# The start of a two-layer kernel on one core: first chunks in halves, products of zeros in TensorE's first waits, and adapter A turned later

## The reference

```
W_b = W0^T + coeff_b * (2 * mask_b - 1)            mask_b: 1024 x 1024 of 0 and 1
y   = x + x W_b + b0
out = y + y W1^T + b1 + (y A_b^T) B_b^T            A_b: 16 x 1024, B_b: 1024 x 16, chosen by ids[b]
```

## Time and profile before

| | us |
|---|---|
| median of 3 runs | 411.49 (410.44 to 413.1) |
| the profiled execution | 411.09 |
| its span, first to last instruction | 409.3 |
| TensorE busy | 396.6 |
| VectorE busy | 283.1 |
| ScalarE busy | 183.8 |

### The profile page before, as it was taken

How to read it: one execution, slowest core, us unless ns; L and a number is a source line. 1 busy time by engine, 2 the same in 40 slices (tenths; PEclk the granted TensorE clock), 3 DMA queues, 4 the chain that set the end, 5 groups by cost and what they waited for, 6 DMA issues and landing times.

```text
span 409.3 us, 6109 instructions
## 1 busy us (share of the span) xinstructions
PE 396.6 (97%) x2358; PEld 364.1 (89%) x2358; DVE 283.1 (69%) x343; ACT 183.8 (45%) x294; POOL 27.4 (7%) x42
## 2 busy tenths in 40 slices
PE   4899999999999999999999999999999999999995
PEld 3787788899999999999999999999999999999994
DVE  1667978867876688577886679575986679575622
ACT  3565675543444344344444345353444334353322
POOL 2224121000001000010001000010001000000000
PEclk9999999999999999999999999999999999999999
DMA  8999986259531893159531893249731793246002
GB/s 282 267 284 270 272 220 172 73 151 254 150 102 57 200 246 98 58 141 246 166 103 56 200 217 110 75 129 216 200 98 49 197 232 107 88 130 168 0 2 103
DMA packets 93633, 63.33 MB, mean 155 GB/s; under 512 B 3612, under 2 KB 90916, under 8 KB 93605
## 3 DMA queue, kind: packets, MB, share of 16 engines
q1 hardware_dynamic: 93586, 62.95, 58.3%
q10 hardware_dynamic: 18, 0.00, 0.0%
HBM read 51.39 MB, written 8.39 MB: 146 GB/s over the span
## 4 chain that ended last, share of the span: by engine, by line
PE 95%; DMA 2%; SPq 1%; DVE 1%; issue 0%; POOL 0%; ACT 0%; DVEq 0%
PE ps L756 29%; PE ps L758 15%; PE ps L802 13%; PE ps L801 13%; PE ps L800 13%; PE ps L734 4%; DMA w0raw<-in_L_cond_W_dram 2%; PE ps L780 2%; PE ps L778 2%; PE ps L779 2%; PE ps L829 2%; PE ps L766 1%; PE ps L811 0%; DVE wm L589 0%; POOL w0raw L341 0%
## 5 line engine op out<-in xcount | busy, mean ns | idle before, releaser
L756 PE MATMUL ps<-xhl,whi 128*128 128x512 f32 x512 | 184.8, 399 | 0.0
L758 PE MATMUL ps<-xhl,wlo 128*128 128x256 f32 x512 | 143.4, 280 | 0.0
L756 PEld LDWEIGHTS ps<-xhl,whi 128*128 128x128 f32 x512 | 96.5, 188 | 20.0 <-DVE xhl L579 0.4
L800 PE MATMUL ps<-w1hi,yhl 128*128 128x344 f32 (+1 forms) x336 | 108.1, 322 | 0.0
L802 PE MATMUL ps<-w1hi,yhl 128*128 128x344 f32 (+1 forms) x336 | 107.7, 321 | 0.0
L801 PE MATMUL ps<-w1lo,yhl 128*128 128x344 f32 (+1 forms) x336 | 107.6, 320 | 0.0
L596 DVE SCALAR_TENSOR_TENSOR wlo<-wm,cs_minus,whi 128x1024 fp32r<-128x1024 f32 x64 | 81.6, 1274 | 25.3 <-ACT whi L421 25.2
L758 PEld LDWEIGHTS ps<-xhl,wlo 128*128 128x128 f32 x512 | 97.0, 189 | 0.3
L421 ACT ACTIVATE whi<-wm,cs_minus 128x1024 fp32r<-128x1024 f32 x64 | 73.7, 1152 | 43.0 <-DVE wm L589 42.9
L589 DVE SCALAR_TENSOR_TENSOR wm<-wm,cs_twice,w0t 128x1024 f32<-128x1024 int32 x64 | 83.8, 1310 | 10.3 <-ACT w0t L402 8.4
L447 ACT ACTIVATE ysum<-ps,b0col 128x256 f32<-128x256 f32 x64 | 30.3, 474 | 85.5 <-PE ps L758 85.3
(11 more groups left out here) (68 smaller groups left out, 217.3 us busy)
## 6 DMA issues: line engine op xcount, KB each, us to landing
wm<-in_mask_Bx4096x_ik_dram SPq DMA_DIRECT2D x64, 512.0 KB, 4.4
xraw<-in_x_dram SPq DMA_DIRECT2D x28, 256.0 KB, 5.8
w0raw<-in_L_cond_W_dram SPq DMA_DIRECT2D x8, 512.0 KB, 7.2
w1raw<-_L_cond_base_weight_dram SPq DMA_DIRECT2D x8, 512.0 KB, 7.4
out_dram<-zst SPq DMA_DIRECT2D x20, 172.0 KB, 2.1
bt<-bhl SPq DMA_DIRECT2D x48, 64.0 KB, 2.3
out_dram<-zst SPq DMA_DIRECT2D x8, 176.0 KB, 2.2
out_dram<-zst SPq DMA_DIRECT2D x8, 164.0 KB, 2.2
```

The source lines that it names most:

```text
L756: nc.tensor.matmul(ps[:, bank, :], whi[:, s, k, :], xhl[:, b % 2, k, :], start=(k == 0), stop=False, skip_group_check=True)
L758: op = nc.tensor.matmul(ps[:, bank, 0:S], wlo[:, s, k, :], xhl[:, b % 2, k, 0:S], start=False, stop=(k == KT - 1), skip_group_check=True)
L800: nc.tensor.matmul(dst, hi, w1hi[:, c, cols], start=(c == 0), stop=False, skip_group_check=True)
```

## The change

- Chunks 0 and 1 are made, rounded and their remainder taken in two halves of 512 columns each (half_make_w, half_chunk_hi, half_chunk_lo), and layer1(0) and (1) wait for each half by itself.
- Twelve products of zeros, 128x128 by 128x512, are issued on TensorE: 5 first, then 2, 2 and 3 between the transposes of the start. Nobody reads them.
- The mask of chunk 0 is loaded ahead of both row blocks of x. The slab W1(0) is turned within chunk 1 of layer 1 and no longer ahead of it, and the order of W1, A, B, the masks, x of batch 1 and the bias on SP's queue changes.
- A is turned at the end of step 2, and adapter_h(0) and (1) run in the middle of layer1(3). B is turned in steps 4 and 5, in place of 3 and 4. A's rows lie in the memory of bt (araw), which GpSimd clears after A has been turned, and the bias is moved after that; B has a tensor of its own (braw).
- y_parts of chunk 2 comes in step 3. The second half of the rows of batch 1 is turned at the end of step 6 and its lo part taken in step 7, ahead of make_y(7).

The diff, cut to its changed lines:

```diff
-         ("w0", 1, 0, 0), ("w0", 1, 1, 1), ("w1", 0, 0, 2), ("w1", 0, 1, 3)]
+         ("w0", 1, 0, 0), ("w0", 1, 1, 1), ("w1", 0, 0, 2), ("w1", 0, 1, 3), ("w0", 2, 0, TB[0]), ("w0", 2, 1, TB[1])]
 for n in range(1, KT):
-    if n + 1 < KT:
+    if 1 < n < KT - 1:
...
+    if n in (4, 5):
+        units.append(("b", 0, n - 4, TB[1]))
+    units += [("w1", n, h, TB[h]) for h in range(2)]
     if n == 2:
-        units += [("a", 0, 0, TB[1]), ("a", 0, 1, HB)]
-    if n in (3, 4):
-        units.append(("b", 0, n - 3, TB[1]))
-    units += [("w1", n, h, TB[h]) for h in range(2)]
+        units += [("a", 0, 0, HB), ("a", 0, 1, TB[0])]
...
 def first_split(st, g):
...
+def first_lo_split(st, g):
+    return 2 * g + st + 1
...
 def l1_bank(n):
...
+    xt_at = nc.sbuf_base
...
+    zeros = nc.alloc_sbuf_tensor_at("zeros", [P, HALF], F32R, offset=xt_at)
...
-    abraw = sb("abraw", [P, D])
+    braw = sb("braw", [P, D])
+    bt_at = nc.sbuf_base
...
+    araw = nc.alloc_sbuf_tensor_at("araw", [P, D], F32, offset=bt_at)
...
         def load_a(adapters):
...
-                sp.dma_start(abraw[e * R:(e + 1) * R, :], src).then_inc(a_in, 16)
+                sp.dma_start(araw[e * R:(e + 1) * R, :], src).then_inc(a_in, 16)
...
         def load_b(adapters):
-            sp.wait_ge(unit_turned, number["a", 0, 1] + 1)
...
-                sp.dma_start(abraw[:, e * P:(e + 1) * P], src).then_inc(b_in, 16)
+                sp.dma_start(braw[:, e * P:(e + 1) * P], src).then_inc(b_in, 16)
...
         def move_bias():
-            sp.wait_ge(consts_set, 1)
+            sp.wait_ge(consts_set, 3)
...
-        sp.dma_start(xrows[:, 0, :], x[0, 0:P, :]).then_inc(rows_in[0], 16)
...
-        sp.dma_start(xrows[:, 1, :], x[0, P:2 * P, :]).then_inc(rows_in[1], 16)
+        for st in range(ST):
+            sp.dma_start(xrows[:, st, :], x[0, st * P:(st + 1) * P, :]).then_inc(rows_in[st], 16)
...
+        load_w1(1)
...
-        load_w1(1)
-        load_a(range(0, 2))
...
+        load_w1(2)
+        load_a(range(0, 4))
...
-        load_a(range(2, 5))
-        load_w1(2)
-        load_a(range(5, NB))
+        load_a(range(4, NB))
...
+            if n == 0:
+                load_b(range(NB))
             if n == 1:
+                load_x(1)
...
-                load_b(range(NB))
-                load_x(1)
...
+        nc.gpsimd.memset(zeros[:, :].bitcast(F32), 0.0).then_inc(consts_set, 1)
+        nc.gpsimd.memset(ht[:, :].bitcast(F32), 1.0).then_inc(consts_set, 1)
...
-        nc.gpsimd.memset(bt[:, :].bitcast(F32), 0.0).then_inc(consts_set, 1)
-        nc.gpsimd.memset(ht[:, :].bitcast(F32), 1.0).then_inc(consts_set, 1)
...
+        eye_w0(4)
...
-        eye_w0(4)
+        pool.wait_ge(unit_turned, number["a", 0, 1] + 1)
+        nc.gpsimd.memset(bt[:, :].bitcast(F32), 0.0).then_inc(consts_set, 1)
...
-                              abraw[:, :].rearrange("p (b o r) -> p o b r", b=NB, o=KT)).then_inc(b_sorted, 1)
+                              braw[:, :].rearrange("p (b o r) -> p o b r", b=NB, o=KT)).then_inc(b_sorted, 1)
...
         def chunk_hi(n):
...
-            if n == 0:
-                act.wait_ge(coeff_made, 2)
...
+        def half_chunk_hi(n, g):
+            if g == 0:
+                act.wait_ge(first_made, n + 1)
+            else:
+                act.wait_ge(w_made, n + 1)
+            k = slice(g * TG, (g + 1) * TG)
+            op = nc.scalar.activation(whi[:, n, k, :], wm[:, n, g * HALF:(g + 1) * HALF].rearrange("p (k o) -> p k o", k=TG),
+                                      ACT.Identity, bias=cs_minus[:, 0:1])
+            if g == 0:
+                op.then_inc(first_hi, 1)
+            else:
+                op.then_inc(w_hi, 1)
...
         def rows_hi(b, g):
...
+        act.wait_ge(coeff_made, 2)
+        half_chunk_hi(0, 0)
...
+        half_chunk_hi(0, 1)
...
-        chunk_hi(0)
...
-        chunk_hi(1)
+        half_chunk_hi(1, 0)
+        half_chunk_hi(1, 1)
...
+            if n == 3:
+                y_parts_hi(2)
...
-            if n == 2:
-                split_hi("a", 0, 0)
-            if n in (3, 4):
-                split_hi("b", 0, n - 3)
+            if n in (4, 5):
+                split_hi("b", 0, n - 4)
...
-            if n == 2:
-                split_hi("a", 0, 1)
-            else:
+            if n != 2:
...
             if n == 2:
-                y_parts_hi(n)
-            if n in (4, 6):
-                rows_hi(1, 3 - n // 2)
+                split_hi("a", 0, 0)
+                split_hi("a", 0, 1)
+            if n in (5, 6):
+                rows_hi(1, 6 - n)
...
+        def half_make_w(n, g):
+            dve.wait_ge(mask_in[n], 16)
+            dve.wait_ge(w0_copied, 2 * n + g + 1)
+            half = wm[:, n, g * HALF:(g + 1) * HALF]
+            op = nc.vector.scalar_tensor_tensor(half, half.bitcast(I32), cs_twice[:, 0:1],
+                                                w0t[:, n, g * TG:(g + 1) * TG, :].rearrange("p k o -> p (k o)"), ALU.mult, ALU.add)
+            if g == 0:
+                op.then_inc(first_made, 1)
+            else:
+                op.then_inc(w_made, 1)
+        def half_chunk_lo(n, g):
+            if g == 0:
+                dve.wait_ge(first_hi, n + 1)
+            else:
+                dve.wait_ge(w_hi, n + 1)
+            k = slice(g * TG, (g + 1) * TG)
+            op = nc.vector.scalar_tensor_tensor(wlo[:, n, k, :], wm[:, n, g * HALF:(g + 1) * HALF].rearrange("p (k o) -> p k o", k=TG),
+                                                cs_minus[:, 0:1], whi[:, n, k, :].bitcast(F32), ALU.add, ALU.subtract)
+            if g == 0:
+                op.then_inc(first_lo, 1)
+            else:
+                op.then_inc(w_lo, 1)
         def make_y(n):
...
-        make_w(0)
+        half_make_w(0, 0)
+        half_make_w(0, 1)
+        half_chunk_lo(0, 0)
...
+        half_chunk_lo(0, 1)
+        first_rows_lo(1, 0)
...
-        chunk_lo(0)
-        first_rows_lo(1, 0)
-        make_w(1)
...
+        half_make_w(1, 0)
+        half_make_w(1, 1)
+        half_chunk_lo(1, 0)
+        half_chunk_lo(1, 1)
...
-        chunk_lo(1)
...
         for n in range(1, KT):
...
+            if n == 3:
+                y_parts_lo(2)
+            if n == KT - 1:
+                rows_lo(1, 0)
...
-            if n == 2:
-                split_lo("a", 0, 0)
-            if n in (3, 4):
-                split_lo("b", 0, n - 3)
+            if n in (4, 5):
+                split_lo("b", 0, n - 4)
...
-            if n == 2:
-                split_lo("a", 0, 1)
-            else:
+            if n != 2:
...
             if n == 2:
-                y_parts_lo(n)
-            if n in (4, 6):
-                rows_lo(1, 3 - n // 2)
-            if n in (3, 5):
-                turn_rows(1, 1 - (n - 3) // 2)
+                split_lo("a", 0, 0)
+                split_lo("a", 0, 1)
+            if n == 5:
+                rows_lo(1, 1)
+            if n in (3, 6):
+                turn_rows(1, 2 - n // 3)
...
-                pe.wait_ge(x_lo, first_split(*units[before[-1]][1:3]))
+                pe.wait_ge(x_lo, first_lo_split(*units[before[-1]][1:3]))
...
-                cut = [abraw[:, (4 * h + m) * P:(4 * h + m + 1) * P] for m in range(4)]
+                cut = [araw[:, (4 * h + m) * P:(4 * h + m + 1) * P] for m in range(4)]
...
-                pe.wait_ge(w_lo, n + 1)
+                if n < 2:
+                    pe.wait_ge(first_lo, n + 1)
+                else:
+                    pe.wait_ge(w_lo, n + 1)
                 if n == 1:
...
+                if n < 2 and k == TG:
+                    pe.wait_ge(w_lo, n + 1)
...
-                    pe.wait_ge(x_lo, first_split(ST - 1, k // TG))
+                    pe.wait_ge(x_lo, first_lo_split(ST - 1, k // TG))
...
+        def idle_products(count):
+            for _ in range(count):
+                nc.tensor.matmul(ps[:, TB[0], :], zeros[:, 0:P], zeros[:, :], start=True, stop=True)
+        pe.wait_ge(consts_set, 1)
+        idle_products(5)
...
-        for st in range(ST):
-            for g in range(2):
-                turn_unit("x", st, g)
-        for h in range(2):
-            turn_unit("w0", 1, h)
+        idle_products(2)
+        turn_unit("x", 0, 0)
+        turn_unit("x", 0, 1)
+        idle_products(2)
+        turn_unit("x", 1, 0)
+        turn_unit("x", 1, 1)
...
+        idle_products(3)
+        turn_unit("w0", 1, 0)
+        turn_unit("w0", 1, 1)
...
-        turn_unit("w1", 0, 0)
-        turn_unit("w1", 0, 1)
         for n in range(1, KT + 1):
-            if n + 1 < KT:
+            if n == 1:
+                layer1(n, range(0, 2))
+                turn_unit("w1", 0, 0)
+                turn_unit("w1", 0, 1)
+                layer1(n, range(2, 4))
+                turn_unit("w0", n + 1, 0)
+                layer1(n, range(4, 6))
+                turn_unit("w0", n + 1, 1)
+                layer1(n, range(6, 8))
+            elif n + 1 < KT:
...
+                if n == 3:
```

(19 more changed lines are left out.)

## The result

| | before | after |
|---|---|---|
| median of 6 runs, us | 411.5 (410.44 to 413.1) | 415.51 (414.6 to 416.03) |
| span of the profiled execution, us | 409.3 | 414.2 |
| TensorE busy in it, us | 396.6 | 401.0 |

The ratio is 1.0087 (95% interval 1.0062 to 1.0113): 4 us slower, where 0.4 us faster was forecast, and outside the range of 408.8 to 413.6 us. The profiled execution after is the slowest of its six (416.03 us), so the spans differ by 4.9 us.

A forecast was written before the change was run, and what follows sets the result against it. TensorE, busy 97% of the span, was taken as the bound, with movable time only ahead of 82 us. Start -1.2, A +0.5, W1(4) -0.3, rows of batch 1 +0.6 gave -0.4: 411.1 us by the median, range 408.8 to 413.6.

The forecast's parts named there:

- Point 5: SP's queue of transfers: W1(4) issued near 39 us and landing at 48 to 50; -0.3 us, ends -0.3 and +1.0.
- A sign of being wrong that the prediction names: TensorE's gaps between 20 and 82 us differing from 1.0 us by over 2.
- rival A: Step 2: GpSimd's bias subtraction starts just ahead of VectorE's remainder of chunk 3 and delays it; 413 us, chance 0.18.
- Theory S: From the experiments: TensorE waits for W1(4) because of what stands ahead on SP's queue, then pays again in pace.
- Point 3: The start up to layer1(1), with zeros, halved chunks and new load order; -1.2 us, ends -2.1 and +0.2.
- the middle case: Start: TensorE's pace rises at about 13.7 us, layer1(1) starts at 18.3; 1.0 us gained.
- the early one: Start: TensorE's pace is full from about 11 us, layer1(1) starts at 17.1 to 17.3; 2.1 us gained.
- Point 4: A turned at the end of step 2, adapter_h(0) and (1) in step 3: moved waits, +0.5 us, ends -0.4 and +2.3.
- Point 6: Batch 1's second half of rows turned in step 6, split in step 7, delaying layer1(8); +0.6 us, ends 0 and 0.9.
- the point against A: In step 2 the remainder of chunk 3 may come first, and then GpSimd waits instead of VectorE.
- B: Rival: at the start the zeros bring full pace before row block 1 is turned; -1.8 us, 409.7 us, chance 0.25.
- C: Rival: at the start the zeros bring no earlier pace and eat the halved chunks' gains; +1.0, 412.5 us, chance 0.12.

The follow-up runs named there:

- e1: The changed kernel with the load of x of batch 1 issued behind W1(4) and its first turning one step later; 412.72 us, 1.0023 of the kernel before.
- e7: The same kernel as e4, run again for a second profile; a single run of 413.31 us.
- e12: e9 (no products of zeros) with VectorE's copy of b0col moved ahead of make_w of chunk 1; 410.81 us, 0.9972 of the kernel before.
- e3: The changed kernel with twelve unused products on TensorE ahead of turning W1(4), to fill the wait; 416.5 us, 1.0107 of the kernel before.
- e2: The changed kernel without its twelve products of zeros; 414.59 us, 1.0088 of the kernel before.
- e5: The changed kernel with W1(2) issued behind A's eight loads and the mask of chunk 3; 414.52 us, 1.0069 of the kernel before.
- e11: e8 with VectorE's copy of b0col moved ahead of make_w of chunk 1; 411.24 us, 0.9978 of the kernel before.
- e6: e5 with x of batch 1 issued behind W1(4) too, as in e1; 412.9 us, 1.0022 of the kernel before.
- e4: The kernel before with only the start changed: halved chunks, zeros, mask ahead of x, W1(0) turned in chunk 1; 412.96 us, 1.0027 of the kernel before.
- e8: e6 with A turned and adapter_h(0) and (1) run in step 2, as before the change; 411.88 us, 0.9997 of the kernel before.
- e9: e8 without the twelve products of zeros; 411.29 us, 0.9980 of the kernel before.
- e10: e8 with the old start: whole chunks, no zeros, old order of x, W1(0) turned ahead of layer1(1); 412.11 us, 0.9991 of the kernel before.

## Why the prediction was wrong, point by point

**Point 5, the queue of transfers, is the step that failed.** It reads "I count W1(4) at 48 to 50: -0.3 us, with ends -0.3 and +1.0". It cost 2.9 us of waiting and 1.6 us of pace, +4.5 in the profile. A sign of being wrong that the prediction names came with it: the gaps between 20 and 82 us are 4.9 us, not 1.0. Three things were wrong in it.
- The issue: 41.41 instead of near 39. I had seen that it waits for the bias and for bt, but counted the bytes ahead of it as if the old hole would swallow them. x of batch 1 is 1 MB, and at the 246 GB/s of the stretch from 36 to 44 us that is an estimated 4.3 us. It had stood ahead of W1(4) before the change too; issuing the slab 0.7 us sooner did not bring it in sooner. e1 took it away and the slab came 3.7 us sooner.
- The need: I judged "just late" against the old 51.47. With the start 2.3 us earlier the need moves to 49.7, and a slab that lands when it did is now a wait. I added a gain in the start to a slab's time as if they were independent. In e7 and e12 they are not: the earlier start waits at the next slab.
- The price: I gave a wait its length. Behind a wait of 3.06 us the clock also fell (1.6 us, against e3), and the diagonal addition, priced at the 0.46 us of the earlier trace rows, met VectorE's remainder and took 1.52. In e2 and e5, where it ran ahead of the remainder, it took 0.45 and 0.46. That is rival A's mechanism at another place.

The Trainium skill (SBUF — State Buffer, "Who interferes with whom") has this as an exclusive lock between a VectorE instruction with two inputs in SBUF and a GpSimd one that reads SBUF. The remainder and the addition are such a pair, and the 1.52 us here and the 1.91 us in e3, where the remainder began 0.01 us ahead, agree with it.

Theory S stands as the account of this wait, but not as I first had it, with the landing fixed by the bytes ahead of the slab. With starts at 16.94, 17.72 and 18.44 the slab was issued at 41.41, 42.74 and 43.85 and landed at 51.1, 52.0 and 54.3 with the same order of transfers. By the code the loads wait on SP's queue for buffers that TensorE frees; that this alone moves the landing was not tested.

**Point 3, the start: the size is right in the mean, and the profile fell outside it.** -1.2 us with ends -2.1 and +0.2. The profile of after has -2.3, over the 2.1 us that the prediction names as a sign of being wrong. It is the earliest of the kernels with zeros: the eight profiles of such kernels (e11, with its copy moved, aside) have starts from 16.94 to 19.17, mean 18.4, so -0.9. Most of them are the middle case, with full pace only for slab 1; after and e6 are the early one. Which of the two an execution meets is not controlled here, and e4 and e7, one kernel, start 0.8 us apart. That the zeros buy the gain is not shown: without them the starts are 17.72, 16.86 and 15.66 (the last with the copy of b0col moved), no later, which points to the halves and the order of transfers, by one profile each.

**Point 4, A: the waits are where I had them; what they cost in the total is not shown.** +0.5 us, made of waits of 1.0 and 0.6. The waits are 0.87 and 0.78, with 0.37 at the second half that I did not have: +0.85 by the profile. After the change they lie ahead of the wait for W1(4), which would have been longer without them; e8 against e6, where that wait is gone, has 1.0 us, with overlapping intervals.

**Point 6, the rows of batch 1: right.** +0.6 us; layer1(8) comes late by 0.35 and layer1(9) by 0.39 more. Two rows of VectorE and TensorE after the change, beside the earlier trace rows:

```profile
79.00 1.27 DVE L622 SCALAR_TENSOR_TENSOR wlo<-wm,cs_minus,whi 128x1024 fp32r<-128x1024 f32 x1
...
80.33 0.50 PE L817 MATMUL ps<-xhl,whi 128*128 128x512 f32 x1
```

Chunk 8's remainder ends at 80.27 and its product starts at 80.33, as I had it in order if not in time.

**The rivals.** A's condition did not hold: the remainder of chunk 3 began at 31.68, 0.83 us ahead of the bias subtraction (32.51), so it was GpSimd that waited, as the point against A said, and the subtraction took 3.24 us instead of 2.37. The remainder took 1.83 us beside the rounding of the bias on GpSimd (1.03 us from 31.39), and that price is inside the 0.85 us of point 4. A's mechanism did its harm at W1(4), where the prediction did not look for it. B's condition held in the one profile of after, full pace ahead of row block 1, and so did its gain at the start; the wait for W1(4) took it back. B and C put their weight on the zeros; without them the time is the same within 2 us (1.0088 against 1.0087), and with A back in its place it is 0.17 points lower (e9 against e8), inside the intervals. A's times are counted from 411.09 us and those of B and C from 411.49; from the median A's case is 413.0 to 415.1 us.

**The sum again.** -2.3 (start), +4.5 (W1(4) and the pace), +0.85 (A), +0.7 (rows of batch 1) make +3.8 of the +4.9 us between the spans; 0.3 us lie ahead of layer1(2), the rest of about 0.8 is in pieces of under 0.5 us, which I have not traced. This adds up marks of two single profiles; by medians the change costs 4.0 us, of which e1 gives back 2.6.

## What to carry to other kernels

When a change speeds up the front of a kernel whose transfers are already just in time, do not add its gain to the sum: move the need of every slab behind it earlier by as much and ask of each whether it is there. On an in-order queue write down the bytes that now stand ahead of the slab that was just late before, and put a load that is needed 30 us later behind it. And a wait of TensorE can cost more than its length: here 1.6 us behind one of 3.06, nothing behind one of 1.60 or of 2.67. Its length alone did not tell which, so read the granted clock behind it.

## What the runs showed of the hardware

- Ahead of the first rise the granted clock in the records does not show the half pace: in the kernel before it reads 1.00 in the first 20 us, where eight transposes take 1.94 to 1.97 us. A fall after that it does show. Two rows of TensorE in e10 and the row of the granted clock on its page, 40 slices of 10.3 us:

```profile
10.82 1.15 PE L788 MATMUL ps<-ident,xrows 128*128 128x128 f32 x8 [1.93 <-DMA xrows<-in_x_dram]
...
13.80 1.94 PE L788 MATMUL ps<-ident,w0raw 128*128 128x128 f32 x8 [1.83 <-POOL w0raw L352]
```

```profile
PEclk9699999999999999999999999999999999999999
```

  The pace had risen by 10.82 and was half again at 13.80: 1.15 and 1.94 us for the same eight transposes, and a granted clock of 0.52 from 12 to 16 us and 0.63 from 16 to 20. It fell between 12 and 13 us (0.57), in the wait. So ahead of the first rise the pace is to be read from the durations.
- The length of a wait did not tell whether the clock would fall. Waits of 1.13 (e5) and 1.60 us (e2) at 50 us and of 2.67 us at 38 us (e12) left it at 1.00. One of 3.06 us was followed by 0.74 and 0.83, and the 1.93 and 1.83 us in e10, with eight transposes between them, by 0.52.
- GpSimd's diagonal addition took 1.52 and 1.91 us where VectorE's remainder had begun 0.06 and 0.01 us ahead of it, and 0.45 and 0.46 us (e2, e5) where the remainder began behind it.
- A DMA share of 1.16 went with 209 GB/s while A's small loads were in flight, and one of 1.12 with 299 in the stretch of the earlier trace rows: a share over 1 went with few bytes and with many. Why small loads cost so much was not measured by itself.
